# TensorE's loop over a gather: two batches and one slot a turn in place of four and two

## The reference

```
x = x + gnn0(layernorm(x))     # 100000 edges: row[src] * weight, summed by dst, then a 256x256 product
x = x + ffn0(layernorm(x))     # router score, top half of the nodes, 256 -> 1024 -> 256 with gelu
x = x + gnn1(layernorm(x))     # 16 relations: (x @ W[rel])[src] * norm * sigmoid gate, summed by dst, relu
x = x + ffn1(layernorm(x))     # 8 experts, top 2, 256 -> 1024 -> 256 with gelu
```

## Time and profile before

| what | value |
|---|---|
| times of three runs | 4026.05, 4010.23, 4010.8 us |
| median | 4010.8 us |
| span of the profiled execution | 3402.6 us |
| median less span | 608.2 us |
| mean granted clock of TensorE | 0.902 |
| mean over the span, DMA | 128 GB/s |

### The profile page before, as it was taken

How to read it: one execution, slowest core, us unless ns; L and a number is a source line. 1 busy time by engine, 2 the same in 40 slices (tenths; PEclk the granted TensorE clock), 3 DMA queues, 4 the chain that set the end, 5 groups by cost and what they waited for, 6 DMA issues and landing times. The chain is left out here.

```text
span 3402.6 us, 59974 instructions
## 1 busy us (share of the span) xinstructions
PE 2615.4 (77%) x14271; PEld 1921.6 (56%) x14272; DVE 1733.1 (51%) x5663; ACT 723.6 (21%) x1907; POOL 1869.7 (55%) x1915
## 2 busy tenths in 40 slices
PE   7688888887777799999655555564555389999997
PEld 6577777776665344444344444443444267767774
DVE  6455545454554655555355454544544544545553
ACT  4121111111110233333211010000000233333332
POOL 1777777777774000000377777777777245555554
PEclk9899999998999899999888888777777689999998
DMA  7333333333332444444545454555544623222232
GB/s 224 110 113 113 113 111 111 113 113 113 110 113 67 173 197 192 188 191 194 194 141 155 151 154 142 152 154 151 146 146 146 241 59 48 45 45 48 45 48 33
DMA packets 175589, 434.08 MB, mean 128 GB/s; under 512 B 41712, under 2 KB 103792, under 8 KB 169232
## 3 DMA queue, kind: packets, MB, share of 16 engines
q0 software_dynamic: 97072, 236.21, 26.9%
q1 hardware_dynamic: 57424, 183.78, 14.1%
q10 hardware_dynamic: 21008, 13.24, 1.3%
HBM read 275.05 MB, written 158.04 MB: 127 GB/s over the span
## 5 line engine op out<-in xcount | busy, mean ns | idle before, releaser
L776 POOL DMA_INDIRECT g_msg<-table,idx x1564 | 1517.3, 970 | 518.8 <-issue 476.5
L848 PE MATMUL psum<-g_msg,g_hot 128*128 x3328 | 967.4, 456 | 593.0 <-SPq L719 358.1
L848 PEld LDWEIGHTS psum<-g_msg,g_hot 128*128 128x128 f32 x3328 | 756.5, 233 | 789.5 <-issue 654.5
L796 DVE TENSOR_SCALAR g_hot<-iota,g_cols 128x128 f32<-128x128 f32 x1664 | 450.1, 364 | 31.9 <-DVE g_cols L793 30.5
L1908 POOL DMA_INDIRECT out<-ex_y,ex_to x112 | 206.0, 1839 | 253.9 <-DMA out<-ex_y,ex_to 165.3
L768 POOL MEMSET g_origin<- 128x256 f32 x1 | 0.3, 313 | 590.8 <-POOLq L1359 590.8
L1594 PE MATMUL psum<-wrel_halves,t_xhi 128*128 128x512 f16 x784 | 298.2, 380 | 1.7 <-DVE t_row L1475 1.7
L1595 PE MATMUL psum<-wrel_halves,t_xhi 128*128 128x512 f16 x784 | 298.1, 380 | 0.0
L1596 PE MATMUL psum<-wrel_halves,t_xlo 128*128 128x512 f16 x784 | 298.1, 380 | 0.0
L1475 DVE TENSOR_SCALAR t_row<-psum,t_gate 128x256 f32<-128x256 f32 x392 | 171.2, 479 | 233.7 <-PE psum L1596 231.7
L2074 PE MATMUL psum<-w,ex_ghi 128*128 x784 | 260.6, 382 | 6.7 <-DVE ex_y L1983 6.4
(11 more groups left out here) (353 smaller groups left out, 3231.7 us busy)
## 6 DMA issues: line engine op xcount, KB each, us to landing
table<-t_row SPq DMA_DIRECT2D x48, 2048.0 KB, 6.3
g_msg<-table,idx POOLq DMA_INDIRECT x1564
piece_stage<-in_w SPq DMA_DIRECT2D x32, 512.0 KB, 5.7
w_halves<-piece_halves SPq DMA_DIRECT2D x32, 512.0 KB, 3.4
w<-w_halves SPq DMA_DIRECT2D x8, 2048.0 KB, 22.6
rows<-sc_row ACTq DMA_DIRECT2D x50, 128.0 KB, 2.2
out<-acc ACTq DMA_DIRECT2D x49, 128.0 KB
table<-t_row SPq DMA_DIRECT2D x24, 256.0 KB, 2.5
```

Source lines behind the costliest of these rows:

```text
L776: pool.indirect_dma_start(out=msg[:, at:at + D], out_offset=None, in_=table, in_offset=bass.IndirectOffsetOnAxis(ap=t[f"idx{g}"][:, n:n + ...
L796: last = nc.vector.tensor_scalar(hot[b][:, k * P:(k + 1) * P], t["iota32"][:, :], c3[:, k, where:where + 1], c3[:, k, weight:weight + 1], ...
L848: pe.matmul(ps, hot[b % PAIR][:, k * P:(k + 1) * P], msg[:, bass.ds(slot_at[k], D)], start=False, stop=False, skip_group_check=True).then_ ...
```

## The change

In `gather`, PE's loop runs `TURNS` (52) times over `PAIR` (2) batches and one slot, where it ran `rounds` (26) times over four batches and two slots. The values waited on for `tiles_in` and for the bank are masked with 1023. The loads of `slot_number` (all three engines that use it) and of the window's number in ACT's `close_from` become `value_load`, which has the check of bounds.

```
-    rounds = STEPS // RING
...
     def slot_number(eng, m):
 
-        _, (n,) = nc.values_load_multi_w_load_instructions(slot_at(m, 0, 1), engines=[eng.engine], min_val=0, max_val=WINDOWS,
-                                                           skip_runtime_bounds_check_because=sure)
-        return n
+        return eng.value_load(slot_at(m, 0, 1), min_val=0, max_val=WINDOWS)
...
-            with pe.Fori(0, rounds) as i:
-                for b in range(BATCHES):
-                    m = BATCHES * i + b
+            with pe.Fori(0, TURNS) as i:
+                for b in range(PAIR):
+                    m = PAIR * i + b
...
-                    pe.wait_ge(tiles_in, code[MSG_TILES])
+                    pe.wait_ge(tiles_in, code[MSG_TILES] & 1023)
...
-                            pe.wait_ge(bank_free, code[BATCH + k // BANKS] + 1)
+                            pe.wait_ge(bank_free, (code[BATCH + k // BANKS] & 1023) + 1)
...
-                    if follow and b % 2:
-                        slots(pe, follow.tensor, 2 * i + b // 2)
+                if follow:
+                    slots(pe, follow.tensor, i)
...
-                    _, (n,) = nc.values_load_multi_w_load_instructions(
-                        t["closed"][0:1, bass.ds(m, 1)], engines=[act.engine], min_val=0, max_val=WINDOWS - 1 - k,
-                        skip_runtime_bounds_check_because=sure)
+                    n = act.value_load(t["closed"][0:1, bass.ds(m, 1)], min_val=0, max_val=WINDOWS - 1 - k)
```

## The result

| | median us | runs | ratio to before, 95% |
|---|---|---|---|
| before | 4010.5 (4004.6 to 4026.1) | 4 | |
| changed | 4048.8 (4037.4 to 4056.8) | 4 | 1.0095 (1.0068 to 1.0122) |

The changed kernel is 38 us slower (27 to 49 by the interval). The forecast was 4012, within 4006 to 4026; it was wrong, and the time lies beyond rival B's 4036.

The account below looks back on a forecast made before the run. POOL's issuing of fetches was taken to bound both gathers, PE's sequencer second in gather 0. Span 3402.6 + 1.0 + 0.1 + 0 = 3403.7 us; the same 1.1 us on the median 4010.8 gave 4012, range 4006 to 4026.

Parts of the forecast that it names:

- rival B: PE's sequencer sets gather 0's pace: 1.04 us per pair, 52 us less 28 of reserve, 4036 us; chance 0.09.
- the total: Whole kernel: profiled span 3402.6 becomes 3403.7 us; the same 1.1 us added to the runs' median 4010.8 gives 4012.
- The reserve: PE's slack in gather 0 that absorbs added sequencer work: 19 to 48 us; gather 1 has waits of 294.8 us.
- The costs of the parts: Added PE sequencer time in gather 0: 0.47 to 0.63 us per pair, 24 to 31 us over 50 pairs.
- masks: Three more register operations per batch on PE's sequencer: together 0.30 to 0.46 us exposed per pair.
- edges: PE's loop closes 52 times per gather, before 26: 0.35 us exposed each, 0.17 us per pair.
- The checks: Checked loads, 0.31 us more each, hidden under PE's running second batch; taken as zero within the pairs.
- Ends of the gathers: Behind the last batches: 1.0 us later after gather 0, 0.1 us after gather 1.
- A: The reserve is used up and gather 0 ends 3 to 12 us late: 4015 to 4024 us; chance 0.18.
- C: Faster: a shorter loop body saves code fetches at back edges, 4010 us, or 3990 if outside the span; chance 0.08.
- D: Nothing shows, masks and checks fall in gaps: 4010.8 us; chance 0.65 together with the forecast.
- What would show it wrong: Signs: POOL waiting for `ring_free`, PE's last-batch wait gone, a pair of 19 us or more, or time the span lacks.

Follow-up runs that it names:

- e4: The changed kernel unaltered, run again beside the kernel before: 3404.0 us, before 3401.9, ratio 1.0007.
- e5: The changed kernel plus one unused checked load per pair of batches on PE: 3454.0 us, 1.0148 of the kernel before.
- e17: The changed kernel unaltered, beside the kernel before (4045.4 us): 4105.8 us, ratio 1.0148.
- e16: The kernel before plus masks and checked loads, keeping four batches and two slots a turn: 4087.2 us, 1.0099 of the kernel before.
- e14: The kernel before plus masks and checked loads, keeping four batches and two slots a turn: 3405.1 us, 1.0001 of the kernel before.

## Why the prediction was wrong

**The step that failed** is the one of the total: "The median of the runs, 4010.8, lies 608.2 us above the span, and the edit has nothing in that part that I could cost". What the runs showed in its place: the surplus lies inside the two gathers (486 and 155 us in the changed kernel), and each run of the experiments, the kernel before's too, has a span some 2 us under its time. I had treated a difference of 18% as something that lies around the span, although nothing in the profile showed such a thing, and so used the reserves of one condition for runs made in another. That the edit would vanish in a reserve was thus right for the trace and wrong for the runs, by 38 us in place of 1.1.

**The reserve.** "The reserve's upper bound is 51.5 x 0.93 = 48 us" is right for the condition of the trace: in e4 PE's waits for landings are 25.7 us less, and e5 breaks through. In the long condition there is next to none, in gather 0 or in gather 1 (2.9 and 0.6 us of PE's waits for landings, for 49.7 and 294.8).

**The costs of the parts were of the right size.** The working had 0.47 to 0.63 us per pair; e4 shows 0.47 (gaps of 2.38 and 1.55 where 2.3 to 2.5 and 1.6 to 1.7 were expected). Unhidden this is 52 pairs x 2 gathers x 0.47 to 0.63 = 49 to 66 us. Measured were 60 us (51 to 68) in e17's series and 38 (27 to 49) in the result's. These two disagree beyond their intervals, and the second reaches the estimate only with its end. In the three long series the kernel before took 4010.5, 4051.9 and 4045.4 us, so the long condition is not one fixed state. By part: masks 104 x 0.30 to 0.46 = 31 to 48 us, measured with the checks 42 (27 to 53); edges 104 x 0.17 = 18 us, measured 18.6 with its wide interval. The checks were taken as nothing; no run has them alone, so that is not shown. The closeness of the edges' number is in part luck: the working counted gaps alone, and in the profiles of e16 and e17 most of the difference is busy time at a lower clock. In the quick condition, with the reserve spent, an edge cost 0.73 us where 0.35 was taken.

**Ends of the gathers.** +1.0 us behind gather 0: it is there, 1.03 us in e4, and too small for the time of a run to show.

**Rivals.** B (4036, chance 0.09) had the mechanism. Its price was an addition of 1.04 us per pair less a reserve of 28 us, in one gather only; the runs have 0.4 to 0.6 us per pair (38 and 60 us over 104 pairs) with next to no reserve, in two gathers. A, C and D fell for the timed runs: no run gained from a shorter body, and in the quick condition nothing depends on where the code lies. In the long condition that was not tried.

**What would show it wrong** named "POOL waiting for `ring_free`, a wait of PE at the last batch that is gone, a pair of 19 us or more": all three stand in the profile with the result (492.1 us; the last batch runs on from the one before, 32 products in one piece from 1554.57 us; a pair of 29.65 us).

**What stays open.** What brings the long condition: the executions with the result and two of the eight series of the experiments had it, and no run could bring it about. What holds the sequencers in steps of 0.7 us, and why the gathers have it and the stretches behind them don't. Every timed run was recorded too (each lists a span and a granted clock), so it isn't shown either whether a sequencer is held at its work or at writing its records. The pauses in line 1063 come after 9 to 26 of its 32 products in the slots from 600 to 700 us, so it is no fixed place in the code. There is no trace of the kernel before in the long condition, only its times; that POOL waits less there by 38 to 60 us is an inference. The Trainium skill, "Runtime: NRT & Kernel Launch", Instruction fetch mechanics, says that a sequencer gets its instructions ahead of time by a DMA queue of its own, and that this is mostly hidden. A slow fetch would fit pauses in straight code and at every kind of instruction. The traces speak against it. They list two DMA queues of the kind "instruction", and these moved as much in the long profile with the result as in the quick one of e4; both pages have these lines:

```profile
q14 instruction: 68, 0.56, 0.0%
q8 instruction: 16, 0.26, 0.0%
```

From 125 us to the end of gather 0 there are 12 such packets in the long profile and 11 in the quick one, and none from 306 to 337 us, where the pauses of the timeline above lie.

## What to carry to other kernels

Set the profiled span beside the timed runs first. Where they differ by far more than the runs among themselves, as here by 608 us, suspect that the profile shows another condition: its durations may hold, its slacks may not, and an addition must also be priced with no slack at all. Here that price, 49 to 66 us, was in the working, and only the hiding was wrong. And in a loop whose pace is within a few per cent of a sequencer's, register operations on that sequencer (here 0.04 to 0.09 us a mask, some 0.36 to 0.73 us a back edge) are the currency, and a gap that they lengthen can cost more than itself where TensorE's granted clock falls behind it (0.87 for 0.93 in e5). A longer body with fewer turns is then the cheaper form, though in the quick condition it made no difference until loads were added.

## What the runs showed of the hardware

- The same kernel on the same chip took 3405 us in one series and 4087 in another (e14, e16). The stretches outside the gathers (relation table 597 and 598 us, experts 733 and 731) don't change; both gathers do (984 to 1470, 994 to 1149 us).
- In the long condition the sequencers of PE, DVE, ACT and SP show maxima near 0.7 and 1.4 us with unchanged medians in the gathers (`SEQ_ASSERT` of line 726, 18 ns in the median, up to 1386), and none in the experts (line 2055, 93 ns at most).
- A gap of PE of 3.04 us (e5) was followed by 4.5 us at the lower level of the clock (0.50); gaps of 2.38 us (e4) were followed by 1.00 once and by 0.60 over 4.3 us once. With the longer gaps gather 0 had a granted clock of 0.87 for 0.93 and 49 us more of busy time for the same products.
- A second mask cost 0.084 us for each operation on a register (0.04 to 0.09), though its own duration is 36 ns (line 843, median).
- 48 more products of PE in front of gather 0 moved its code without an effect in the quick condition (1.0005, 0.9995 to 1.0015).
